# Gathering a mixture's result by batch, inside the attention that follows it

## The reference, cut to what matters

```python
x = x + mamba(layernorm(x))
x = x + ffn(layernorm(x))            # 32 experts, top 4
x = x + attn_rotary(layernorm(x))
x = x + ffn(layernorm(x))            # the same experts again
...
# in ffn, after the experts: outs has one row for each (token, choice)
outs = outs[inv].reshape(-1, K, Hh)                     # K = 4
y = jnp.sum(outs * topk_weight[..., None], axis=1)
# in attn_rotary: qkv = x @ w_atten.T; rope on q, k; causal softmax(q k / 4) v; @ w_proj.T
# layernorm: (x - mean) / sqrt(var + 1e-5), over the 256 features of one token
```

## Time and profile before

| | us |
|---|---|
| median of 3 runs | 4024.61 (4023.0 to 4031.77) |
| the profiled execution, as timed | 4027.84 |
| its span in the trace | 4025.8 |
| first gather of the first `combine` | 832.0 |
| last statistics of that `combine` | 917.4 |
| first maximum of the attention's loop (unit 0) | 949.5 |
| last statistics of the attention | 1341.7 |

### The profile page before, as it was taken

One profiled execution on the slowest core, in us unless ns is written; L12 is line 12 of the kernel. 1 busy time (PEld: TensorE's weight loads), 2 busy tenths in 40 slices (PEclk: granted clock), 3 DMA queues, 4 the chain that ended last, 5 costly groups with the idle time before them and its releaser, 6 DMA issues. The chain is left out here.

```text
span 4025.8 us, 68076 instructions
## 1 busy us (share of the span) xinstructions
PE 3274.6 (81%) x19700; PEld 2587.2 (64%) x19707; DVE 2799.5 (70%) x6227; ACT 2271.6 (56%) x5958; POOL 1766.8 (44%) x3039
## 2 busy tenths in 40 slices
PE   7799977926888599079999999999956399999574
...
GB/s 87 19 49 47 50 154 84 137 104 22 1 1 1 149 114 132 102 48 20 18 9 20 17 10 19 17 12 19 16 189 66 114 1 1 1 1 1 163 71 112
DMA packets 139502, 221.36 MB, mean 55 GB/s; under 512 B 28960, under 2 KB 114848, under 8 KB 137456
## 3 DMA queue, kind: packets, MB, share of 16 engines
...
...
## 5 line engine op out<-in xcount | busy, mean ns | idle before, releaser
L1261 POOL DMA_INDIRECT ex_xr<-scratch_rows,mo_token x288 | 287.0, 997 | 325.9 <-PE bank L1320 167.0
L610 POOL TENSOR_TENSOR sc_h<-sc_h,sc_c 128x512 f32<-128x512 f32 x256 | 326.9, 1289 | 197.6 <-DVE sc_h L647 189.4
L3051 DVE TENSOR_TENSOR sa_pT<-bank,sa_pT 128x512 fp32r<-128x512 f32 x512 | 329.9, 686 | 34.0 <-ACT sa_pT L2922 30.2
L2914 ACT ACTIVATE sa_p<-bank,sa_nm 128x512 f32<-128x512 f32 x512 | 346.7, 688 | 2.4 <-DVE sa_nm L3042 2.4
L647 DVE TENSOR_TENSOR_SCAN sc_h<-sc_da,bank 128x512 f32<-128x512 f32 x256 | 311.1, 1220 | 38.1 <-ACT sc_da L590 23.2
L2743 PE MATMUL bank<-sa_kT,sa_qT 128*128 128x512 f32 x1024 | 333.6, 437 | 1.5 <-DVE residual L3018 1.5
L3038 DVE TENSOR_REDUCE sa_mx<-bank 128x2 f32<-128x1024 f32 x256 | 312.2, 1220 | 26.3 <-PE bank L2745 22.2
L2767 PE MATMUL bank<-sa_pT,sa_v 128*128 128x256 f32 x2048 | 300.9, 290 | 16.8 <-DVE sa_pT L3051 16.4
L1338 PE MATMUL bank<-mo_w_gu,ex_xT 128*128 (+2 forms) x1152 | 310.4, 397 | 1.0 <-issue 0.8
L2767 PEld LDWEIGHTS bank<-sa_pT,sa_v 128*128 128x128 f32 x2048 | 260.3, 189 | 39.7 <-DVE sa_pT L3051 29.5
L2922 ACT ACTIVATE sa_pT<-bank 128x512 fp32r<-128x512 f32 x512 | 274.3, 585 | 7.8 <-PE bank L2755 0.6
...
## 6 DMA issues: line engine op xcount, KB each, us to landing
scratch_ys<-ex_yo SPq DMA_DIRECT2D x192, 128.0 KB, 2.2
mo_w_gu<-in_w_gu SPq DMA_DIRECT2D x2, 9216.0 KB, 26.4
...
sa_share<-scratch_shares SPq DMA_DIRECT2D x256, 64.0 KB, 2.6
...
mo_w_dn<-in_w_dn SPq DMA_DIRECT2D x2, 4096.0 KB, 34.6
...
```

Of the source, the lines that this page charges most:

```text
L610: pool.tensor_tensor(h, h, C[u], ALU.mult).then_inc(used.sem, 1)
L1261: pool.indirect_dma_start(xr[u][:, :], None, rows, bass.IndirectOffsetOnAxis(ap=token[:, i:i + 1], axis=0), bounds_check=rows.shape[0] - 1 ...
L2914: act.activation(pr[h][:, :], SC[2 * s_ + h][:, :], ACT.Exp, bias=nm[:, col:col + 1], scale=SCALE, accum_out=rs[:, col:col + 1]).then_inc( ...
L3051: dve.tensor_tensor(spot(1), PT[h][:, :].rearrange("p (k n) -> p k n", k=TPB), spot(0).bitcast(F32), ALU.subtract).then_inc(*inc("kept_d"))
```

## The change

The first mixture no longer calls `combine`. Its slots and weights are handed to `rotary`, whose block now holds the gathering too. POOL gathers batch 0 (16 DMAs) first, into 8 buffers instead of 16; the other 48 gathers stand between POOL's later instructions, at places from two tables (`FETCH`), and DVE's weighted adds (`mix`) between its units (`MIX`): for batch 1 one in each unit from 2 to 17; for batch 2 in groups 2 to 4 and for batch 3 in groups 6 to 8, six in a group, one in every second unit from unit 4 on (four in the last). Each tile's statistics follow its fourth mix. Mean and variance are computed batch by batch (`statistics`, for batches 1 to 3 in unit 3 of groups 1, 5 and 9), and POOL raises the variance to the power -0.5 where ACT and DVE took root and reciprocal. The zeroing of `qT` and `v` moves from POOL to DVE. The second mixture, after the attention, still uses `combine`.

```diff
@@ combine / moe @@
-        if cap is None:
+        if cap is None and shares is None:
             combine(c, K, NT * ROWS, ys, slots, weights)
@@ rotary @@
-def rotary(c):
+def rotary(c, slots, weights):
...
+        def gather(pool, n):
+            u = n % NB
+            if n >= NB:
+                pool.wait_ge(mixed.sem, mixed.at(n - NB + 1))
+            pool.indirect_dma_start(YB[:, u * D_MODEL:(u + 1) * D_MODEL], None, ys,
+                                    bass.IndirectOffsetOnAxis(ap=slots[:, n:n + 1], axis=0),
+                                    bounds_check=SLOTS - 1, oob_is_err=False).then_inc(fetched[u].sem, 16)
+
+        def mix(dve, n):
+            u, i = n % NB, n // K
+            at_x = c.x[:, i * D_MODEL:(i + 1) * D_MODEL]
+            dve.wait_ge(fetched[u].sem, fetched[u].at(16 * (n // NB + 1)))
+            if n % K:
+                dve.wait_ge(mixed.sem, mixed.at(n))
+            dve.scalar_tensor_tensor(out=at_x, in0=YB[:, u * D_MODEL:(u + 1) * D_MODEL], scalar=weights[:, n:n + 1],
+                                     in1=at_x, op0=ALU.mult, op1=ALU.add).then_inc(mixed.sem, 1)
+
+        NS = TPB * K
+        EARLY = 8
+        FETCH, MIX = {}, {}
+        for j in range(EARLY, NS):
+            FETCH.setdefault((0, min((j - EARLY) // 3, 2)), []).append(NS + j)
+        for j in range(NS):
+            MIX.setdefault(divmod(2 + j, UNITS), []).append(NS + j)
+            for b in range(2, BATCH):
+                FETCH.setdefault((G * (b - 2) + 1 + j // 6, TPB - 1), []).append(b * NS + j)
+                MIX.setdefault((G * (b - 2) + 2 + j // 6, 4 + j % 6 * 2), []).append(b * NS + j)
+        STAND = {(G * (b - 1) + 1, 3): b for b in range(1, BATCH)}
@@ POOL @@
+                for n in range(NS):
+                    gather(pool, n)
                 pool.memset(mask[:, :], 0.0).then_inc(*inc("made"))
...
-                for u in range(2):
-                    for hh in range(HG):
-                        rows = slice(WR, P) if hh % 2 == 0 else slice(0, WR)
-                        pool.wait_ge(*at("made", 4 + u * HG + hh))
-                        pool.memset(qT[u][rows, hh * SEQ:(hh + 1) * SEQ].bitcast(F32), 0.0).then_inc(*inc("made"))
-                for u in range(4):
-                    pool.memset(vv[u][:, :].bitcast(F32), 0.0).then_inc(*inc("made"))
...
+                def root(b):
+                    cut = slice(b * TPB, (b + 1) * TPB)
+                    pool.wait_ge(*at("own", 7 * (b + 1) + (8 if b else 0)))
+                    pool.tensor_tensor(rstd[:, cut], var[:, cut], power[:, :], ALU.pow).then_inc(*inc("root"))
+
+                root(0)
+                for j in range(5):
+                    gather(pool, NS + j)
...
                 put_group(0, (0, 1))
                 pool.sem_inc(sig["qput"].sem, 2)
+                for j in range(5, EARLY):
+                    gather(pool, NS + j)
                 put_group(1, range(TPB))
                 for I in range(NG + 1):
-                    if I + 2 < NG:
-                        put_group(I + 2, range(TPB - 1))
-                    if I >= 1:
-                        add_parts(I - 1)
-                    if I + 2 < NG:
-                        put_group(I + 2, (TPB - 1,))
+                    for i in range(TPB):
+                        if i == TPB - 1 and I >= 1:
+                            add_parts(I - 1)
+                        if I + 2 < NG:
+                            put_group(I + 2, (i,))
+                        if i == 0 and (I, 3) in STAND:
+                            root(STAND[I, 3])
+                        for n in FETCH.get((I, i), ()):
+                            gather(pool, n)
@@ PE @@
-                pe.wait_ge(*at("made", 4 + 2 * HG))
+                pe.wait_ge(*at("made", 4))
+                pe.wait_ge(*at("cleared", 2 * HG))
@@ ACT @@
-                act.wait_ge(*at("own", 7))
-                act.activation(tmp[:, :], var[:, :], ACT.Sqrt).then_inc(*inc("root"))
@@ DVE @@
+                for u in range(2):
+                    for hh in range(HG):
...
+                        dve.memset(qT[u][rows, hh * SEQ:(hh + 1) * SEQ].bitcast(F32), 0.0).then_inc(*inc("cleared"))
+                for n in range(NS):
+                    mix(dve, n)
+                    if n % K == K - 1:
+                        clear(n // K)
+                        dve.wait_ge(mixed.sem, mixed.at(n + 1))
+                        tile_stats(c, dve, n // K, "at_own_k")
+                statistics(0)
                 dve.wait_ge(*at("root", 1))
-                st.then(dve.reciprocal(rstd[:, :], tmp[:, :]))
...
+                    for n in MIX.get((I, r), ()):
+                        mix(dve, n)
+                        if n % K == K - 1:
+                            dve.wait_ge(mixed.sem, mixed.at(n + 1))
+                            tile_stats(c, dve, n // K, "at_own_k")
+                    if (I, r) in STAND:
+                        statistics(STAND[I, r])
```

62 lines of the change are left out of this document (41 added, 21 removed).

## The result

| | before | after |
|---|---|---|
| median of the runs, us | 4027.84 (4 runs: 4023.0 to 4031.77) | 3999.46 (4 runs: 3996.89 to 4001.53) |
| profiled execution, us | 4027.84 | 3996.89 |
| its span | 4025.8 | 3994.8 |
| 16th gather to the end of the attention's loop (maximum of unit 255) | 470.7 | 440.3 |

The ratio is 0.9933, 95% interval 0.992 to 0.9945: faster by 28 us in the medians, by 31.0 in the spans, of which 30.4 lie between the 16th gather and the end of the loop. The prediction was 3988 (3970 to 4006), and the median lies some 11 us above it. 3.2 of the 11 come from the base: the forecast took 3.2 off because the profiled execution lay 3.2 above the median of three runs, and with a fourth run of the kernel before the median is where that execution is, at 4027.84.

The account below looks back on a forecast made before the run. POOL's pace set the gathering; in the attention's loop no engine was full, they hand units to one another. 63.3 - 9.7 - 14.9 - 2.2 = 36.5 us gained, taking the median from 4024.6 to 3988 us, range 3970 to 4006.

Parts of the forecast that it names:

- to R: From the gathering to R, the end of POOL's last put that PE awaits in unit 4 (957.80 before): 63.3 us gained.
- R to the start of group 2: Groups 0 and 1 after unit 4's wait: late gathers and batch 1's statistics lose 9.7 us, bounds 5.7 and 13.
- mixes and tile statistics of batches 2, 3: In the attention's loop, 18.6 us of DVE work at a factor of 0.8: 14.9 us lost, bounds 0 to 24.7.
- their batch statistics: The other two batch statistics on DVE: 2 x (1.9 - 0.8) = 2.2 us lost, bounds 0 and 3.8.
- POOL must issue eight gathers between the four puts: 26.1 us: In group 2's puts: 4 x 3.93 + 8 x 1.303 = 26.1 us, where PE wants the result after 20.4: 5.7 late.
- factor of 0.8: In the loop's groups: the share of DVE's added mix and tile-statistics time that a group pays, giving 14.9 us lost.
- Clock: PE's clock: 0.92 in group 0, 1.00 afterwards; half-speed stretches at new waits set at 0, up to 3 us in the range.
- DVE's gaps hide the mixes: Rival, in the loop: idle DVE time covers the mixes, only POOL's 5.7 us is lost: 3967 us, chance 0.14.
- POOL and DVE lock each other: Rival, in group 0: each mix holds POOL for its full length, 7.2 us lost: 3995 us, chance 0.12.
- the 0.16 of the earlier trace: In group 0: a POOL product takes 0.48 us beside DVE's puts, 0.32 alone; 16 mixes would cost POOL 2.6 us.
- The chain of units is tighter: Rival: every DVE delay passes to PE and ACT and back: mixes 24.7, statistics 3.8, start 13; 4003 us, chance 0.20.
- POOL falls behind: Rival, in the loop: every mix waits for its own gather, so the 62.5 saved come back: 4048 us, slower, chance 0.05.

Follow-up runs that it names:

- no_late_gather1: The kernel after without the last 8 gathers of batch 1, which POOL issues between its puts in group 0; their mixes stay and read old rows: median 3991.4 us.
- no_mix1: The kernel after without batch 1's 16 mixes in units 2 to 17; their gathers and statistics stay: median 3999.1 us.
- mix_behind_wait: The kernel after with batch 1's last two mixes moved from units 16 and 17 to units 18 and 19: median 3992.0 us.
- no_mix23: The kernel after without the 32 mixes of batches 2 and 3; their gathers and statistics stay: median 3988.8 us.
- gather_before_root: The kernel after with three of batch 1's gathers moved ahead of the power on POOL: median 3990.0 us.
- no_gather23: The kernel after without the 32 gathers of batches 2 and 3; their mixes stay and read rows already there: median 3998.5 us.

## Why the prediction was right, and where its sizes were off

The range held the time and the order of events was as told. Of the signs under "right" these appeared: the first normalized tile near 860, the DVE memset ahead of it, the longer wait in unit 4, and groups 2 and 3 near 25.5 us. Two held in part: DVE waited for its gather in unit 16 and not in unit 17, and from group 10 on all was as before, but group 9 grew by 1.8, which the prediction's own sum has as batch statistics. By its steps, in us of the profiled execution (gains positive):

| step | predicted | measured | by |
|---|---|---|---|
| to R | 63.3 | 62.5 | PE row at 895.31 against the earlier trace rows |
| R to the start of group 2 | -9.7 | -13.6 | windows; no_late_gather1, no_mix1, mix_behind_wait |
| mixes and tile statistics of batches 2, 3 | -14.9 | -16.1, some 0.8 of it clock | windows of groups 2 to 4, 6 to 8; no_mix23 |
| their batch statistics | -2.2 | -3.1, 0.45 of it clock | windows of groups 5, 9 |
| elsewhere | 0 | +1.3 | span |
| sum | 36.5 | 31.0 | |

**To R.** Right in size. The 48 gathers are the gain. Statistics and power take 858.07 to 860.76, 2.7 us as forecast, and the memset 1.87 + 0.40 against 2.3. That it costs nothing elsewhere was right as well, but the 5.10 us that POOL idles ahead of the power were overlooked: gather_before_root shows that they were worth 3.9.

**R to group 1.** The 13.6 lost lie just beyond the step's outer bound of 13. The step "POOL must issue eight gathers between the four puts: 26.1 us" was too short by 3.7: POOL needs 29.8 (895.45 to 925.21). It left out the turns: ahead of a gather behind a put POOL idles 0.9 to 1.2 us, where 0.2 lie between two puts, 1.9 more in all. And beside the mixes the four puts take 16.6 us instead of 4 x 3.73, 1.7 more. So the mix of unit 16 waits until R + 26.0 instead of R + 22.4, and unit 17 comes 10.5 late where 7.8 was forecast. Its sum has a slip as well: 7.8 for the wait and 1.9 for the statistics are 9.7 before the 0.8 that it means to subtract, and 8.9 after. The step's second assumption, that batch 1's other mixes lie inside the wait, holds only in part: in units 5 to 15 they cost 5.1 us one by one, part of which the wait then repays; no_mix1, where units 5 to 15 take 1.2 us more than before instead of 5.1, puts the sum of all 16 at 4.6. And the 0.8 us of DVE's idle time in unit 19 can't hide the statistics, since they stand behind the `low_v` that waits. Another 1.0 is lost in units 4 and 5 (R moved by 62.5, unit 5 by 61.5): half of it is PE at half clock, where 0 was set with up to 3 in the range (four transposes in 1.11 us and not 0.66), half the mix that stands between (no_mix1 reaches unit 5 0.5 earlier).

**Mixes of batches 2 and 3.** The factor of 0.8 was measured at 0.83 for the mixes (11.9 us against 14.4 x 0.8 = 11.5), or 0.77 without the clock's share. The tile statistics came out at their full 0.53 each. What was wrong is to think of the factor as a property of the loop. It is one of the place: in units 0 to 3 of four groups the same 18.6 us of mixes and tile statistics cost 2.3, in their old place 15.3. The prediction had seen both facts, the idle time ahead of unit 4 and the mixes behind it, and used them only to choose a number.

**Clock.** The prediction had 1.00 from group 1 on and set 0 for the clock. Group 1 ran at 0.86, and stretches at half clock fell into seven of the groups 2 to 9, at a price of some 1.2 us there.

**Batch statistics.** 1.38 us each in unit 3, seven instructions at 0.2; the 0.8 subtracted for idle time was again time ahead of them.

**The rivals.** "DVE's gaps hide the mixes" is refuted for the places that the change chose and nearly true for others. "POOL and DVE lock each other" for the length of a mix does not hold: group 2's four puts, with nine mixes beside them, lost 1.7 us, some 0.19 for a mix and not 0.45, so the 0.16 of the earlier trace rows was the right size. It was weighed as a rival and then left out of the sum, though. 0.19 us beside a mix of 0.47 is milder than the exclusive lock that the Trainium skill (SBUF — State Buffer, Who interferes with whom) describes. "The chain of units is tighter" would have cost 24.7 us in groups 2 to 4 and 6 to 8, and they lost 16.1; nearest to it came the start, with 13.6 lost where it has 13 for that stretch, by POOL's lateness and the mixes together. "POOL falls behind" never came near: from group 2 on the waits show no mix that waited for a gather, and no_gather23 shows that POOL's extra work there costs nothing.

What stays open: what PE's clock, at 0.82 in group 0 (0.88 in no_mix1), costs in units 5 to 15, which no run separates; what brings the stretches at half clock later on; and where the 1.3 us outside the stretch come from.
